# Cross-attention and expert feed-forward on one core: the probabilities' transpose goes from TensorE to a DMA

## The reference

```python
def _L0_xattn_ref(x, context, tgt_mask, src_mask, Wq, Wk, Wv, Wo, bo):   # x normalized, (4, 1024, 512); context (4, 64, 512)
    q, k, v = ...                       # 16 heads of 64
    sim = jnp.einsum('bhid,bhjd->bhij', q, k) * SCALE
    sim = jnp.where(tgt_mask == 0, neg, sim)
    sim = jnp.where(src_mask[:, None, :], sim, neg)
    attn = jax.nn.softmax(sim, axis=-1)
    out = jnp.einsum('bhij,bhjd->bhid', attn, v)
    ...
    return jnp.einsum('bne,oe->bno', out, Wo) + bo

x = x + _L0_xattn_ref(_layernorm(x), ctx_1024, ...)
x = x + _L0_ffn_ref(_layernorm(x), ...)   # a shared ReLU net plus one of two expert nets, chosen per row
```

## Time and profile before

| | |
|---|---|
| median of 3 runs | 1856.94 us (1856.17 to 1858.8) |
| the profiled execution | 1857.37 us, of which span 1855.7 us |
| busy: PE, DVE, ACT, POOL | 98%, 43%, 44%, 27% of the span |
| granted TensorE clock, mean | 0.996 |
| attention's loop over tiles | 106 to 481 us |

### The profile page before, as it was taken

How to read it: one execution, slowest core, us unless ns; L and a number is a source line. 1 busy time by engine, 2 the same in 40 slices (tenths; PEclk the granted TensorE clock), 3 DMA queues, 4 the chain that set the end, 5 groups by cost and what they waited for, 6 DMA issues and landing times.

```text
span 1855.7 us, 33404 instructions
## 1 busy us (share of the span) xinstructions
PE 1816.3 (98%) x11516; PEld 1145.4 (62%) x11517; DVE 797.8 (43%) x1651; ACT 820.8 (44%) x1441; POOL 509.2 (27%) x475
## 2 busy tenths in 40 slices
PE   8989999999999999999999999999999999999997
PEld 6334444544566666666666666666666666666664
DVE  6987778777344333343433333222222222222222
ACT  4655555555333333334444444333333343333333
POOL 2047777777101111211100011312211221221210
PEclk9999999999999999999999999999999999999999
DMA  9246555655932332323444493921111122121100
GB/s 330 86 95 158 161 164 165 177 165 137 296 130 81 99 95 82 100 80 125 126 156 138 142 332 105 264 55 46 47 46 45 39 57 54 51 61 47 46 24 15
DMA packets 225955, 214.44 MB, mean 116 GB/s; under 512 B 126635, under 2 KB 168140, under 8 KB 225484
## 3 DMA queue, kind: packets, MB, share of 16 engines
q1 hardware_dynamic: 216924, 188.09, 34.4%
q0 software_dynamic: 8944, 25.19, 4.4%
HBM read 129.57 MB, written 59.02 MB: 102 GB/s over the span
## 4 chain that ended last, share of the span: by engine, by line
PE 88%; DVE 5%; POOL 2%; issue 2%; DMA 1%; ACT 1%; SPq 0%; POOLq 0%; DVEq 0%; ACTq 0%
PE pS L1081 36%; PE pP L1093 18%; PE pG L1093 9%; PE pO L1093 9%; PE pO L485 7%; PE banks_a L464 4%; PE pS L464 3%; DVE seen L799 2%; DVE room_w L819 1%; PE pP L474 1%; POOL room_b L659 1%; POOL room_b L654 1%; DMA e_split<-room_b 0%; POOL room_a L344 0%; PE banks_a L507 0%
## 5 line engine op out<-in xcount | busy, mean ns | idle before, releaser
L1081 PE MATMUL pS<-room_a,room_w 128*128 128x256 f16 (+1 forms) x6336 | 765.0, 271 | 1.5 <-issue 1.1
L1081 PEld LDWEIGHTS pS<-room_a,room_w 128*128 (+1 forms) x6336 | 611.2, 98 | 182.1 <-issue 10.2
L1112 DVE TENSOR_TENSOR room_a<-room_a 128x256 f16<-128x256 f32 (+1 forms) x528 | 237.6, 450 | 906.3 <-ACT room_a L1106 894.9
L1093 PE MATMUL pP<-room_w,room_a 128*128 (+1 forms) x1584 | 383.5, 379 | 0.1
L1104 ACT ACTIVATE room_a<-pS,room_b,sc 128x256 f32<-128x256 f32 (+1 forms) x272 | 151.7, 558 | 420.4 <-PE pS L1081 395.7
L1104 ACT ACTIVATE room_a<-pS,b1s,sc 128x256 f32<-128x256 f32 x256 | 144.2, 563 | 370.0 <-PE pS L1081 365.2
L1093 PEld LDWEIGHTS pP<-room_w,room_a 128*128 128x128 f16 x1584 | 154.8, 98 | 132.2 <-issue 0.7
L1093 PE MATMUL pG<-room_w,room_a 128*128 128x512 f16 (+1 forms) x768 | 207.6, 379 | 0.5 <-DVE room_a L1112 0.5
L1093 PE MATMUL pO<-room_w,room_a 128*128 128x512 f16 (+1 forms) x768 | 207.5, 379 | 0.0
L1128 POOL TENSOR_TENSOR room_a<-room_a,room_b 128x512 f32<-128x512 f32 x32 | 42.7, 1354 | 516.6 <-DVE room_a L1119 516.6
L485 PE MATMUL pO<-room_w,room_b 128*128 (+1 forms) x768 | 174.4, 384 | 7.6 <-DVE room_b L703 7.5
(11 more groups left out here) (180 smaller groups left out, 1540.8 us busy)
## 6 DMA issues: line engine op xcount, KB each, us to landing
room_b<-in_w SPq DMA_DIRECT2D x64, 512.0 KB, 5.0
e_split<-room_b SPq DMA_DIRECT2D x64, 256.0 KB
room_w<-e_split SPq DMA_DIRECT2D x8, 2048.0 KB
rows_room<-in_x SPq DMA_DIRECT2D x32, 256.0 KB, 3.1
room_a<-in_sw SPq DMA_DIRECT2D x32, 256.0 KB, 4.2
room_b<-in_x SPq DMA_DIRECT2D x32, 256.0 KB, 3.8
s_split<-room_a SPq DMA_DIRECT2D x64, 128.0 KB, 3.7
x_scratch<-room_b SPq DMA_DIRECT2D x32, 256.0 KB, 4.0
```

Of the source, the lines that this page charges most:

```text
L1081: mm = q.matmul(self.pH[j % 2][:, 0:rows], w[:, k, j * P:(j + 1) * P], zt[:, u, k, 0:rows], start=(n == 0), stop=(n == 3 * KC - 1))
L1093: mm = q.matmul(self.pY[u][r][:, :], h[:, j % self.HR, r * P:(r + 1) * P], w[:, j, :], start=(j == 0 and n == 0), stop=(j == HC - 1 and n ...
L1112: q.tensor_tensor(self.hl[:, j % self.HR, 0:rows], self.hf[:, j % self.HR, 0:rows], self.hh[:, j % self.HR, 0:rows], ALU.subtract).then_in ...
```

## The change

Probabilities are no longer transposed on TensorE. `norm` still leaves them in `s`, not transposed. ScalarE writes their high half, scaled, as float16 to a new SBUF buffer `prs[:, 0]`, and then the same scaled product once more in float32 to PSUM (`scaled`, the bank that `pP` had). VectorE subtracts the one from the other into `prs[:, 1]`. One transposing DMA (`turn_p`) turns the 128x2048 float16 of `prs`, 512 KB, into `pT`, which has two buffers; `prs` has one. `attend` reads `pT`. Everything up to `turn_p` is done one pass earlier than the transposed halves were: `hi_p`, `lo_p` and `turn_p` in pass t are for tile t+1. On DVE the sums go behind the statistics, shifts and `pick`, and `lo_p` to the end of the pass; POOL's and ACT's orders are changed as well. The identity matrix and its set-up are gone, some buffers of the later phases lie elsewhere, and VectorE waits for z of tile 30 ahead of its first writes of the shared net.

```diff
+                    def turn_p(e, g, u):
+                        e.wait_ge(S["pl"], count(g, u))
+                        at_least(e, S["att"], count(g, u) - 2)
+                        e.dma_start(pT[:, u % 2, :, :], prs[:, :, :, :].rearrange("p l h k -> p (l h k)"), transpose=True).then_inc(S["pT_in", u % 2], 16)
...
                             step(sp, g, u, -2, store_z)
+                            step(sp, g, u, 1, turn_p)
...
-                    def t_p(e, g, u):
-                        e.wait_ge(S["prob"], count(g, u))
-                        at_least(e, S["pTl"], count(g, u) - 1)
-                        for q in range(PAIRS):
-                            mm = e.transpose(pP[:, q * P:(q + 1) * P],
-                                             s[:, u % 2, 2 * q:2 * q + 2, :].rearrange("p h k -> p (h k)"), ident[:, :])
-                        mm.then_inc(S["pT"], 1)
-
                     def attend(e, g, u):
-                        e.wait_ge(S["pTl"], count(g, u))
+                        e.wait_ge(S["pT_in", u % 2], dma_count2(g, u))
                         at_least(e, S["x1"], count(g, u) - 1)
...
                     def hi_p(e, g, u):
-                        e.wait_ge(S["pT"], count(g, u))
-                        at_least(e, S["att"], count(g, u) - 1)
-                        e.activation(pTh[:, :, :], pP[:, :].rearrange("p (k n) -> p k n", k=PAIRS), ACT.Copy, scale=P_SCALE).then_inc(S["pTh"], 1)
+                        e.wait_ge(S["prob"], count(g, u))
+                        if u > 0:
+                            e.wait_ge(S["pT_in", (u - 1) % 2], dma_count2(g, u - 1))
+                        elif not isinstance(g, int) or g > 0:
+                            e.wait_ge(S["pT_in", 1], 32 * g)
+                        e.activation(prs[:, 0, :, :], s[:, u % 2, :, :], ACT.Copy, scale=P_SCALE)
+                        at_least(e, S["pl"], count(g, u) - 1)
+                        e.activation(scaled, s[:, u % 2, :, :], ACT.Copy, scale=P_SCALE).then_inc(S["ph"], 1)
...
                         for u in range(N):
-                            step(act, g, u, 0, hi_p)
                             step(act, g, u, 1, exp)
...
                             if not early(g, u, 4):
                                 step(act, g, u, 4, normal)
+                            step(act, g, u, 1, hi_p)
...
                     def lo_p(e, g, u):
-                        e.wait_ge(S["pTh"], count(g, u))
-                        e.scalar_tensor_tensor(out=pTl[:, :, :], in0=pP[:, :].rearrange("p (k n) -> p k n", k=PAIRS), scalar=P_SCALE,
-                                               in1=pTh[:, :, :], op0=ALU.mult, op1=ALU.subtract).then_inc(S["pTl"], 1)
+                        e.wait_ge(S["ph"], count(g, u))
+                        e.scalar_tensor_tensor(out=prs[:, 1, :, :], in0=scaled, scalar=1.0,
+                                               in1=prs[:, 0, :, :], op0=ALU.mult, op1=ALU.subtract).then_inc(S["pl"], 1)
...
                             if first_tile(g, u, 2):
                                 step(pool, g, u, 4, lo_x)
+                            step(pool, g, u, 2, low_w)
                             step(pool, g, u, 1, norm)
+                            step(pool, g, u, -1, lo_z)
                             step(pool, g, u, 2, sub)
-                            step(pool, g, u, 2, low_w)
-                            step(pool, g, u, -1, lo_z)
...
+                            step(dve, g, u, 1, sums)
                             step(dve, g, u, 2, masked)
...
+                            step(dve, g, u, 1, lo_p)
...
+        dve.wait_ge(z_done, SUB - 1)
```

More of the change, by code:

```diff
@@ L951, in xattn_ffn @@
                 is0 = take([SLOT_TILES])
-                order = take([SLOT_SUBS])
-                iz = take([Net.N, Net.R], I32)
-                flags, needs = (take([SLOT_TILES], I32) for _ in range(2))
-                ir, io = (take([Net.N, Net.R], I32) for _ in range(2))
-                bsel = take([Net.N, HC])
+                order = late_take([SLOT_SUBS])
+                iz = late_take([Net.N, Net.R], I32)
+                flags, needs = (late_take([SLOT_TILES], I32) for _ in range(2))
+                ir, io = (late_take([Net.N, Net.R], I32) for _ in range(2))
+                bsel = late_take([Net.N, HC])
                 picks = (flags, needs, ir, io, bsel)
@@ L1015, with __init__ @@
     LAG = 2
-    def __init__(self, tag, count, sem, sc, ident, a1, a2, room, rows_room, banks, half=None):
-        self.tiles, self.ident, self.half = count, ident, half
+    def __init__(self, tag, count, sem, sc, a1, a2, room, rows_room, banks, half=None):
+        self.tiles, self.half = count, half
         self.a1, self.a2 = sc[:, a1:a1 + 1], sc[:, a2:a2 + 1]
```

64 lines of the change are left out of this document (25 added, 39 removed).

## The result

The changed kernel takes 1874.06 us, the median of 4 runs (1870.34 to 1874.89), against 1857.38 for the kernel before beside it (1856.17 to 1858.8). The ratio is 1.0086, with a 95% interval of 1.0073 to 1.0098. It is slower by about 0.9%, and outside the range. The profiled execution of the changed kernel is the run of 1870.34, with a span of 1868.6 us; the span before was 1855.7, so the trace has 12.9 us to explain.

The account below looks back on a forecast made before the run. VectorE's relay and z's late store, not TensorE, were to set the pass at 11.1 us; loop -6.7, head +3.0 and tail +3.0 made -0.7 us, so 1856.2 us on the median, range 1845 to 1868.

Parts of the forecast that it names:

- the loop: 28 attention passes, residual of tile 0 to that of tile 28: 11.1 us each against 11.34, -6.7 us.
- the head: Up to tile 0's residual: `norm`(0) to `attend`(0) grows from 4.5 to 7.5 us, +3.0 us; the rest keeps its length.
- the tail: From tile 28's residual to the shared net's first matmul: `turn_p`(31) stands ahead of its loads, +3 us, between 0 and +5.
- the pass: Mean time of one attention pass, (10.85 + 11.4) / 2 = 11.1 us, where PE needs 10.36.
- C: Time from a residual's start to the next issue of `turn_p`, forecast as 10.85 us.
- Z: Time from `turn_p`'s issue through SP's queue to the residual waiting for z's store: 11.4 us, bounds 10.95 and 12.0.
- The bound now: TensorE bounds the kernel before: a pass is 11.23 us without a gap, 0.87 of it transposes.
- the relay: Chain in one pass: `sums`, `norm` on GpSimd, two ScalarE activations, `lo_p` at 9.6 us, next residual at 10.8.
- 9.2 us of work: VectorE's work in one pass of the kernel before, 282.34 to 291.97 less 0.45 of waiting.
- the formula: Mean pass = (C + Z) / 2, as the two limits take turns or share the delay.
- 9.07 + 2.9 - 0.6 = 11.4: Today's `turn_x`-to-residual time, plus the new 512 KB transpose's DMA work, less 0.6 us of queue gaps filled.
- The late-store rival: z's store lands later still, Z 12.0, pass 11.5: +10.5 us, 1867.4 us, slower; decides from Z = 11.7; chance 0.28, including a long tail.

Follow-up runs that it names:

- the short relay: Changed kernel with stores of x1 and z issued first in SP's pass, VectorE's passes written out, and `sums`, `norm`, `hi_p` moved earlier: 1842.36 us, ratio 0.9916.
- the store alone: Changed kernel with the stores of x1 and z issued first in SP's pass, right behind `turn_p`: 1863.17 us, ratio 1.0026.

## Why the prediction was wrong

The forecast of 1856.2 was low by 17.9 us at the median. At the profiled run (1856.7 against 1870.34) it was low by 13.6: 6.7 in the loop, 3.6 in the head, 0.4 in the tail, 2.9 in parts that were given nothing. The step that failed first is the pass: the two limits C and Z, forecast at 10.85 and 11.4 us, measured 11.18 and 11.71, and the loop's gain of 6.7 us was gone. The second is the head, where two terms stood at nothing. Step by step:

- **The bound now and the relay (right).** PE's pass, the order of the relay and each of its steps held. `lo_p` waited 1.65 us (forecast 1.5) and the relay took 10.81 to 10.99 us, 10.85 on average (10.8), where VectorE's passes are written out.
- **The relay inside the hardware loop (missed).** The prediction took one C for all passes, 10.85. Measured from the residual to `turn_p`'s issue, C was 10.95 with VectorE written out and 11.18 on average in the changed kernel. The term that failed is "9.2 us of work" from rows of the kernel before, whose end the loop makes later by up to 0.7 us a pass here. Why those rows don't hold it is argued, not shown: there `lo_p`, with its wait for ScalarE, stood between the residual and the statistics and can have covered it. By the formula, 28 x 0.33 / 2 = +4.6 us.
- **Z (mechanism right, size off).** The term "9.07 + 2.9 - 0.6 = 11.4" measured 11.71. The 2.9 us of work was right, as two kernels with early stores show: in the 28 passes the DMA share times the pass was 0.91 x 10.36 = 9.4 us with the short relay, and 0.58 x 11.23 = 6.5 in the kernel before with early stores, 2.9 apart for 512 KB. That is 180 GB/s. The rule of 350 to 400 GB/s that the prediction cites from the Trainium skill's page "Advanced Engine Details and Errata" ("X-Bar Transpose (TRN2)") does not hold for this transpose. The 2.3 that the prediction added to 9.07 measured 2.65: 1.79 for `turn_p`'s issue, 0.58 more from `turn_x`'s issue to the store's, which `turn_x`'s own longer issue covers (1.91 against 1.24 on average), and 0.28 more from the store to the residual. By the formula, 28 x 0.31 / 2 = +4.3 us.
- **C and Z together (sizes only bounded).** They make +8.9 by the formula, while the loop missed its 11.125 a pass by 6.2 us (6.7 from the rounded 11.1). The formula gives 11.44 for the changed kernel, where 11.345 was measured: it lets every residual wait for z, and only 8 did. How the miss divides between the two is open. What lifting each gives is measured: nothing for the hardware loop alone, 7.4 us for the store alone, 13.9 for both.
- **The late-store rival** named the right mechanism and the right sign, 0.28. Z came out at its threshold of 11.7 and under its bound of 12.0. The error was to hold the other limit fixed at 10.85 while only Z was let vary.
- **Head (missed by half).** +3.0 was the longer way from `norm`(0) to `attend`(0), and that measured 7.7 against 4.5, +3.2. Two terms had been set to nothing. `norm`(0) ended 1.3 us later; in the short relay, which puts it ahead of `low_w` again, `attend`(0) started 0.9 us earlier, so the order explains most of it. And `attend`(0) took 7.4 us to its residual instead of 5.4, since the longer idle time ended in the clock's lower level: +2.0. The prediction named that clock step for the tail and not for the head.
- **Tail (right, with luck).** +3.4 against +3.0. The issues came as forecast (`turn_p`(31), z transposes and weights at R + 20.2, 22.1 and 27.0 against 20.6, 22.4 and 27.1), but +3.0 was only the middle between two bounds. The weights landed within 7.0 us of their issue, not 8.6. The last `attend` took 8.1 us, not 5.3, its first 5.5 us at a granted clock of 0.50 behind 4.1 us of idle time, and ended at R + 33.1, 0.8 ahead of the first matmul. The two errors offset each other.
- **The start and the rest** (+1.2 and +1.7) are not explained. The first score matmul started between 106.3 and 108.1 us in the other kernels too, those made from the kernel before among them, so the 1.2 can be what varies from one execution to the next.
- **Left open:** three of the four runs of the changed kernel lie at 1874 to 1875, 3.7 us above the profiled one. No trace shows those.

## What to carry to other kernels

When a change takes work from the bounding engine, write down the longest relay of the other engines, step by step, and ask where in their orders each of its steps stands: here moves of order alone turned a loss of 0.9% into a gain of 0.9%. Two limits that lie side by side must be lifted together: one of them lifted alone gave no gain at all, the other half of what both gave. Where the bounding engine gets a new idle stretch, price what it does after it at the lower clock, in the head of a loop as well as in its tail.

## What the runs showed of the hardware

- A relay across engines took longer when VectorE's part ran as a hardware loop: 10.81 to 10.99 us written out against 11.01 to 11.53 in the loop. With 0.9 us of slack it cost nothing (290.39 against 290.08 us for 28 passes).
- A transposing DMA's issue on SP depended on what was queued ahead: for `turn_x` 1.24 us in the kernel before, 1.77 in the median in the changed kernel, where another transposing DMA stands ahead, and for a 512 KB one 7.18 instead of 1.79 behind 2 MB of plain loads.
- A transposing DMA of 512 KB from SBUF to SBUF added 2.9 us of work on the 16 DMA engines to a pass, 180 GB/s.
- VectorE and GpSimd, both reading SBUF with VectorE on two SBUF operands, took turns: 2.93 and 2.14 us instead of 1.23 and 1.16. With one operand in PSUM, VectorE's operation took 1.23 beside GpSimd's.
- 36 matmuls without use in an idle stretch of 8.6 us kept the clock at 1.00 and gave back 1.6 us of the attend behind it.
